# Norm stages of a graph network: one more 128x256 product behind each sum on TensorE, and a ring of sums of three pairs

## The chip, the core and the metric

The kernel runs on one core of a Trainium2 chip. The metric is the device time of one execution in microseconds (us): 6430.47 us is the median of three runs. TensorE appears as PE in the views (its weight loads as PEld), VectorE as DVE, ScalarE as ACT, GpSimd as POOL, SyncE as SP. The granted clock of TensorE is a share of full speed: 1.00 is 2.4 GHz, 0.50 is 1.2 GHz.

## The reference, cut to what matters

A layer of graph convolutions with four Runge-Kutta steps, then an attention layer. There are 50000 nodes, 25000 edges sorted by their destination, and rows of 128 or 256 numbers.

```python
def _gcn_conv(x, W, b, src, dst, dinv):
    h = x @ W
    norm = dinv[src] * dinv[dst]
    agg = jax.ops.segment_sum(h[src] * norm[:, None], dst, num_segments=x.shape[0])
    agg = agg + (dinv * dinv)[:, None] * h
    return agg + b
def f(z):
    z1 = _gcn_conv(z, Wf1, bf1, src, dst, dinv)
    z1 = _l2norm(z1)
    return _gcn_conv(z1, Wf2, bf2, src, dst, dinv) + z
k1 = f(x)
k2 = f(x + 0.5 * k1)
k3 = f(x + 0.5 * k2)
k4 = f(x + k3)
x = x + (k1 + 2.0 * k2 + 2.0 * k3 + k4) / 6.0
return _gcn_conv(x, W2, b2, src, dst, dinv)
...
x = _layernorm(x + _L0_gnn_ref(...), axis=-1)
x = _layernorm(x + _L1_gnn_ref(...), axis=-1)
```

Each `segment_sum` over 25000 edges becomes a row of small products: a 0/1 matrix that says which edges of a tile of 128 belong together (`sums_all`) times the 128 gathered rows of the tile.

## The kernel before, in words

The program is a row of stages with a barrier between them: preparation, a local pass over nodes without edges, then `first_stage`, and then by turns five norm stages (`norm_stage`, r = 0 to 4) and four mix stages (`mix_stage`, r = 0 to 3), and at the end the attention. Each norm and mix stage goes over the same 196 edge tiles, two at a time: 98 pairs. A norm stage with r = 0 to 3 has rows of 256 numbers; r = 4 (the final one) has rows of 128. In the timing, norm stage r = 0 lies at about 2088 to 2443 us, r = 1 at 2804 to 3160, r = 2 at 3521 to 3876, r = 3 at 4239 to 4682 and r = 4 at 4998 to 5290.

Work of a norm stage for pair j, tiles i = 0 and 1:

- POOL gathers the rows of both tiles from HBM into `c_rows`, a ring of four pairs (`gather_step`, L1398, two indirect DMAs); the gather of pair j waits until the sums of pair j-4 are done. Every second pair POOL also makes an inverse root (`invert`, L1735).
- SP issues the loads of `c_degs`, `c_own` and, in r = 1, 2 and 4, of one more table, in r = 3 of three more (`load_others`, L1718).
- DVE adds the last row of the sum before to the first row of the tile (`carry_step`, L1390), since a node's edges can run over a tile's border. This is the chain of the stage: the carry of tile t needs the sum of tile t-1, and the sum of tile t needs its carry.
- PE makes the sum (`add_up`): first a bias product without a wait on the carry (L1752, a single pass in the trace), then a wait for `carried`, then the 128x256 product with `sums_all` (L1754, 32-bit floats, two passes in the trace). The two accumulate in one PSUM bank. The banks are used in turn: tile 2j+i has bank (2j+i) mod 8, four pairs.
- DVE takes the pair's sums out of PSUM and adds the own rows (`add_own`, L1832) in the turn behind, clamps (L1845), and in r = 1 to 3 scales and adds an earlier table (`add_t`, L1859); ACT squares (L1773), in r = 0 also scales, and stores the pair.

DVE takes its work in the order in which it is written: carry of tile 0, `add_own` of the pair before, carry of tile 1, then the rest.

Of the kernel before, what the change touches and what calls it, by code (L numbers as in the profile page):

```python
# [13 lines left out]
D, H2 = 128, 256  # L14
# [1272 lines left out]
def coupled_stages(nc, a, S, counts, m):  # L1287
# [9 lines left out]
    with ctx:  # L1297
# [25 lines left out]
        for r in range(4):  # L1323
            norm_stage(nc, S, counts, m, r)
            if r < 3:
                mix_stage(nc, S, counts, m, r)
        mix_stage(nc, S, counts, m, 3)
        norm_stage(nc, S, counts, m, 4)


def two(tile, s, w):

    return tile[:, s, 0:2 * w].rearrange("p (i c) -> p i c", i=2)
# [18 lines left out]
def spread_turn(nc, S, m, line):  # L1352

    for k, tiles_ in enumerate((P, TE - P)):
        last = nc.tensor.transpose(m["psum"][7][0:tiles_, k * P:(k + 1) * P], line[:, k * P:k * P + tiles_],
                                   m["ident"][:])
    last.then_inc(S["degs_turned"], 1)


def spread_high(nc, act, S, m, begun):  # L1360

    act.wait_ge(S["degs_turned"], begun + 1)
    for k, tiles_ in enumerate((P, TE - P)):
        last = nc.scalar.activation(m["c_deg_hi"][0:tiles_, k, :], m["psum"][7][0:tiles_, k * P:(k + 1) * P], ACT.Copy)
    last.then_inc(S["degs_split"], 1)
# [11 lines left out]
def bias_of(m, name):  # L1377
    return m["bias_rows"][:, BIAS_AT[name][0]:BIAS_AT[name][1]]


def carry_step(nc, dve, S, m, st, before, w, i, j):


    p0, t = (0, 96)[i], 2 * j + i
    if t == 0:
        dve.sem_inc(S["carried"], 1)  # L1386
        return
    dve.wait_ge(S["summed"], st.at("summed", t))
    rows = two(m["c_rows"], j % 4, H2)[p0:p0 + 32, i, 0:w]
    nc.vector.scalar_tensor_tensor(rows, before[p0:p0 + 32, :], m["carry"][p0:p0 + 32, t:t + 1], rows, ALU.mult, ALU.add  # L1390
                                   ).then_inc(S["carried"], 1)
# [283 lines left out]
def norm_stage(nc, S, counts, m, r):  # L1675
# [4 lines left out]
    w = D if final else H2  # L1680
# [5 lines left out]
    v, psum = nc.vector, m["psum"]  # L1686
    own, rows, sums, y, rest = (m[n] for n in ("c_own", "c_rows", "sums_all", "c_y", "c_rest"))
# [4 lines left out]
    st = Steps(counts, {"carried": 2 * pairs, "summed": 2 * pairs, "u_set": pairs, "squared": 0 if final else pairs,  # L1692
                        "clamped": pairs // 2, "inverted": pairs // 2, "done": pairs,
                        "rest_set": 2 * pairs if r == 3 else 0, "x_added": pairs if final else 0,
                        "chain": 2 * pairs if final else 0, "shifted": pairs if final else 0},
               {"gathered": (32, 4, pairs), "own_in": (16, 4, pairs), "degs_in": (16, 4, pairs),
                "others_in": (16 * len(others), 4, pairs), "stored": (16, 8, pairs)})
    READY = 7

    with nc.Block() as block:  # L1700
        @block.sync
        def _(sp):
            def load(j):
                if j >= 4:
                    sp.wait_ge(S["u_set"], st.at("u_set", j - 3))
                sp.dma_start(flat(own, j % 4, w), pair_rows(source, j)).then_inc(S[st.sem("own_in", j)], 16)

            def load_degs(j):
                if j >= 4:
                    sp.wait_ge(S["summed"], st.at("summed", 2 * j - 6))  # L1710
                sp.dma_start(degs[0:3, j % 8, :].bitcast(F32), m["kap_tab"][:, j * 2 * P:(j + 1) * 2 * P]
                             ).then_inc(S[st.sem("degs_in", j)], 16)

            def load_others(j):
                if j >= 4:
                    sp.wait_ge(S["x_added" if final else "done"], st.at("x_added" if final else "done", j - 3))
                for n, table in enumerate(others):
                    sp.dma_start(flat(zs[n], j % 4, w), pair_rows(table, j)).then_inc(S[st.sem("others_in", j)], 16)  # L1718

            if r == 0:  # L1720
                spread_out(sp, S, m, m["kap_tab"], 1)
            late = 3 if final else 6
            for turn in range(pairs + late):
                if turn < pairs:
                    load_degs(turn)
                    load(turn)
                if others and 0 <= turn - late < pairs:
                    load_others(turn - late)
# [15 lines left out]
        @block.tensor  # L1744
        def _(pe):
            def add_up(j, i):
                out = psum[(2 * j + i) % 8][:, 0:w]
                if i == 0:
                    pe.wait_ge(S[st.sem("degs_in", j)], st.landed("degs_in", j))
                    if j >= 4:  # L1750
                        pe.wait_ge(S["u_set"], st.at("u_set", j - 3))
                nc.tensor.matmul(out, degs[:, j % 8, i * P:(i + 1) * P], bias_of(m, bias), start=True, stop=False)  # L1752
                pe.wait_ge(S["carried"], st.at("carried", 2 * j + i + 1))
                nc.tensor.matmul(out, sums[:, 2 * j + i, :], two(rows, j % 4, H2)[:, i, 0:w], start=False, stop=True  # L1754
                                 ).then_inc(S["summed"], 1)

            if r == 0:
                pe.wait_ge(S["kappa_set"], 3)
                spread_turn(nc, S, m, m["c_kappa"])
            for j in range(pairs):  # L1760
                add_up(j, 0)
                add_up(j, 1)

        @block.scalar
        def _(act):
# [11 lines left out]
            def scale(j):  # L1777
                act.wait_ge(S["inverted"], st.at("inverted", j // 2 + 1))
                for i in range(2):
                    part = two(y, j % 8, H2)[:, i, :]  # L1780
                    last = nc.scalar.activation(part, part, ACT.Copy, scale=inv[:, j % 8, i:i + 1])
                last.then_inc(S["done"], 1)

            def normalise(j):
                act.wait_ge(S["shifted"], st.at("shifted", j + 1))
                for i in range(2):
                    part = two(y, j % 8, D)[:, i, :]
                    last = nc.scalar.activation(part, part, ACT.Identity, bias=m["c_shift"][:, j % 2, i:i + 1],
                                                scale=inv[:, j % 8, i:i + 1])
                last.then_inc(S["done"], 1)  # L1790

            def store(j):
                act.wait_ge(S["done"], st.at("done", j + 1))
                act.dma_start(pair_rows(target, j), flat(y, j % 8, w)).then_inc(S[st.sem("stored", j)], 16)

            if r == 0:
                spread_high(nc, act, S, m, 1)
            for turn in range(pairs + READY + 1):
                if r == 0 and 0 <= turn - READY < pairs:
                    scale(turn - READY)  # L1800
                if final and 0 <= turn - READY < pairs:
                    normalise(turn - READY)
                if 0 <= turn - READY < pairs:
                    store(turn - READY)
# [6 lines left out]
        def _(dve):  # L1811
# [9 lines left out]
            def carry(j, i):  # L1821
                if i == 0:
                    dve.wait_ge(S[st.sem("gathered", j)], st.landed("gathered", j))
                carry_step(nc, dve, S, m, st, m["psum"][(2 * j + i - 1) % 8][:, 0:w], w, i, j)

            def add_own(j):
                dve.wait_ge(S["summed"], st.at("summed", 2 * j + 2))
                dve.wait_ge(S[st.sem("own_in", j)], st.landed("own_in", j))
                if j >= 8:
                    dve.wait_ge(S[st.sem("stored", j)], st.landed("stored", j - 8))  # L1830
                for i in range(2):
                    last = v.scalar_tensor_tensor(two(y, j % 8, w)[:, i, :], psum[(2 * j + i) % 8][:, 0:w],  # L1832
                                                  m["lead"][:, 2 * j + i:2 * j + i + 1], two(own, j % 4, w)[:, i, :],
                                                  ALU.mult, ALU.add)
                last.then_inc(S["u_set"], 1)
# [1056 lines left out]
```

## Time and profile before

| what | value |
|---|---|
| median of three runs | 6430.47 us (6430.21 to 6433.66) |
| the profiled execution | 6431.79 us, of which the span from the first to the last instruction is 6429.9 us |
| mean granted TensorE clock over the span | 0.809 |
| PE busy | 5150.1 us (80%) |
| DVE busy | 4720.9 us (73%) |
| POOL busy | 3923.0 us (61%) |
| ACT busy | 2819.0 us (44%) |

A busy share is a mean over stages that have different limits, so the table says where to look and not what bounds. PE's time counts a product from its start to its modelled end, in which the next one may already stream; two products that overlap count once.

### The profile page before, as it was taken

What the parts mean: (1) busy time and instruction counts of PE and PEld (TensorE: products, weight loads), DVE (VectorE), ACT (ScalarE), POOL (GpSimd) and SP (SyncE); (2) the same over time, 40 slices, a digit from 0 to 9 for tenths busy, and PEclk for the clock granted to TensorE, in tenths of its full rate; (3) what the DMA queues carried; (4) which work ended last, traced back from release to release, by engine and by line L of the source; (5) the groups of instructions that cost most, each with busy time, mean ns of one, the idle gap of its engine ahead of it and who ended that gap; (6) DMA issues with size and microseconds to landing.
All of it is one profiled execution on the core that took longest, in us unless ns stands there. A gap on an engine that the chain in (4) does not pass through costs nothing. (4 is left out here: it accounts for less than half of the span.)

```text
span 6429.9 us, 101948 instructions
## 1 busy us (share of the span) xinstructions
PE 5150.1 (80%) x25772; PEld 4128.5 (64%) x25772; DVE 4720.9 (73%) x14274; ACT 2819.0 (44%) x8831; POOL 3923.0 (61%) x3976
## 2 busy tenths in 40 slices
PE   7499999995777778987799778976679558967776
PEld 3389999994766446854487446853368447755654
DVE  8467777775665456867687776878878788888886
ACT  7167777773444553322233222322223236644442
POOL 1277777777554665557655765555556776566664
PEclk9699999997999557965599558965589559989897
DMA  0289988874554667988898888989989555534342
GB/s 2 43 218 261 262 254 258 263 234 129 158 163 156 209 216 258 323 264 287 263 324 283 285 288 280 323 294 341 341 268 282 165 163 162 160 124 122 122 124 79
DMA packets 930902, 1406.59 MB, mean 219 GB/s; under 512 B 157981, under 2 KB 453981, under 8 KB 930355
## 3 DMA queue, kind: packets, MB, share of 16 engines
q1 hardware_dynamic: 664979, 898.20, 43.7%
q0 software_dynamic: 138368, 296.57, 17.1%
q10 hardware_dynamic: 127008, 205.58, 8.7%
q8 instruction: 215, 3.52, 0.2%
q14 instruction: 332, 2.72, 0.1%
HBM read 852.92 MB, written 547.19 MB: 218 GB/s over the span
## 5 line engine op out<-in xcount | busy, mean ns | idle before, releaser
L1390 DVE SCALAR_TENSOR_TENSOR c_rows<-bank,carry,c_rows 32x256 f32<-32x256 f32 (+2 forms) x1950 | 888.6, 456 | 899.2 <-PE bank L1754 506.0
L1754 PE MATMUL bank<-c_rows,sums_all 128*128 128x256 f32 (+1 forms) x1960 | 1112.4, 671 | 532.7 <-DVE c_rows L1390 516.1
L1398 POOL DMA_INDIRECT c_rows<-y_tab,src_pair x784 | 757.0, 966 | 602.2 <-PE bank L1754 382.4
L1754 PEld LDWEIGHTS bank<-c_rows,sums_all 128*128 128x128 f32 x1960 | 489.8, 310 | 965.9 <-DVE c_rows L1390 948.3
L1398 POOL DMA_INDIRECT c_rows<-t_tab,src_pair x784 | 741.1, 945 | 519.8 <-PE bank L1982 360.6
L1773 ACT ACTIVATE c_squares<-c_y,c_root 128x256 f32<-128x256 f32 x784 | 391.7, 500 | 1022.8 <-DVE c_y L1859 779.9
L1752 PE MATMUL bank<-bias_rows,c_degs 128*128 128x256 f32 (+1 forms) x980 | 695.6, 710 | 26.7 <-DMA c_degs<-kap_tab 26.7
L2025 ACT ACTIVATE c_xt<-bank 128x512 f32<-128x512 f32 x392 | 234.1, 597 | 906.2 <-PE bank L1991 906.2
L760 PE MATMUL bank<-w_mix,lxt 128*128 128x256 f32 x2400 | 607.3, 381 | 1.9 <-ACT lxt L1029 1.9
L760 PE MATMUL bank<-w_mix,c_xt 128*128 128x256 f32 x2352 | 605.9, 380 | 0.0
L761 PE MATMUL bank<-bias_rows,two_r 128*128 128x256 f32 (+1 forms) x1400 | 595.2, 427 | 0.0
L1982 PE MATMUL bank<-c_rows,sums_all 128*128 128x256 f32 x1568 | 498.6, 400 | 106.3 <-DVEq L1386 81.8
L761 PE MATMUL bank<-bias_rows,c_degs 128*128 128x256 f32 (+1 forms) x1372 | 578.0, 423 | 0.0
L2527 POOL DMA_INDIRECT out_dram<-fl_y,node_of x396 | 394.3, 996 | 243.2 <-DVE fl_y L2845 147.2
L760 PEld LDWEIGHTS bank<-w_mix,c_xt 128*128 128x128 f32 x2352 | 424.8, 191 | 45.9
L760 PEld LDWEIGHTS bank<-w_mix,lxt 128*128 128x128 f32 x2400 | 413.0, 191 | 42.9 <-ACT lxt L1029 3.1
L1048 ACT ACTIVATE lsquares<-ly 128x256 f32<-128x256 f32 x800 | 324.4, 408 | 162.7 <-DVE ly L1219 160.6
L1752 PEld LDWEIGHTS bank<-bias_rows,c_degs 128*128 128x128 f32 x980 | 329.1, 336 | 98.4 <-DMA c_degs<-kap_tab 28.0
L1832 DVE SCALAR_TENSOR_TENSOR c_y<-bank,lead,c_own 128x256 f32<-128x256 f32 (+1 forms) x980 | 390.3, 434 | 2.2 <-PE bank L1754 2.1
L760 PE MATMUL bank<-w_first,c_z 128*128 128x256 f32 (+1 forms) x1176 | 301.4, 357 | 101.1 <-DVE c_y L1653 101.1
L1982 PEld LDWEIGHTS bank<-c_rows,sums_all 128*128 128x128 f32 x1568 | 245.5, 194 | 152.5 <-DVEq L1386 84.7
L2072 DVE SCALAR_TENSOR_TENSOR c_y<-bank,c_scale,c_rest 128x256 f32<-128x256 f32 (+1 forms) x784 | 317.4, 447 | 27.2 <-PE bank L761 15.2
(388 smaller groups left out, 13010.8 us busy)
## 6 DMA issues: line engine op xcount, KB each, us to landing
c_z<-t_tab SPq DMA_DIRECT2D x490, 256.0 KB
y_tab<-ly SPq DMA_DIRECT2D x400, 256.0 KB
t_tab<-lt SPq DMA_DIRECT2D x400, 256.0 KB
c_own<-y_tab SPq DMA_DIRECT2D x392, 256.0 KB
t_tab<-c_y ACTq DMA_DIRECT2D x392, 256.0 KB
c_own<-t_tab SPq DMA_DIRECT2D x392, 256.0 KB
c_z<-y_tab SPq DMA_DIRECT2D x294, 256.0 KB
y_tab<-c_y ACTq DMA_DIRECT2D x294, 256.0 KB
```

Of the source, the lines that this page charges most:

```text
L760: nc.tensor.matmul(out, x(k), w(k), start=(k == 0), stop=False)
L761: return nc.tensor.matmul(out, bias[0], bias[1], start=False, stop=True)
L1048: last = nc.scalar.activation(squares[:, squared[0] % 2, i, :], source(j, i), ACT.Square, scale=scale, accum_out=ss[:, turn % 4, at:at + 1])
L1390: nc.vector.scalar_tensor_tensor(rows, before[p0:p0 + 32, :], m["carry"][p0:p0 + 32, t:t + 1], rows, ALU.mult, ALU.add).then_inc(S["carrie ...
L1398: pool.indirect_dma_start(out=two(m["c_rows"], j % 4, H2)[:, i, 0:w], out_offset=None, in_=source, in_offset=bass.IndirectOffsetOnAxis(ap= ...
L1752: nc.tensor.matmul(out, degs[:, j % 8, i * P:(i + 1) * P], bias_of(m, bias), start=True, stop=False)
L1754: nc.tensor.matmul(out, sums[:, 2 * j + i, :], two(rows, j % 4, H2)[:, i, 0:w], start=False, stop=True).then_inc(S["summed"], 1)
L1773: last = nc.scalar.activation(m["c_squares"][:, i, :], two(y, j % 8, H2)[:, i, :], ACT.Square, scale=root[:, 2 * j + i:2 * j + i + 1], acc ...
L1832: last = v.scalar_tensor_tensor(two(y, j % 8, w)[:, i, :], psum[(2 * j + i) % 8][:, 0:w], m["lead"][:, 2 * j + i:2 * j + i + 1], two(own, ...
L1982: nc.tensor.matmul(psum[j % 2][:, i * H2:(i + 1) * H2], sums[:, 2 * j + i, :], two(rows, j % 4, H2)[:, i, :], start=True, stop=True).then_ ...
L2072: last = v.scalar_tensor_tensor(two(y, j % 8, w)[:, i, :], psum[4 + j % 2][:, i * H2:i * H2 + w], m["c_scale"][:, 2 * j + i:2 * j + i + 1] ...
L2527: pool.indirect_dma_start(out=m["out"], in_=y[:, j % 4, i, :], in_offset=None, out_offset=bass.IndirectOffsetOnAxis(ap=m["node_of"][:, t:t ...
```

## The change

Behind each sum in the norm stages PE gets one more product of 128x128 by 128x256 (`ident` times the first 256 columns of `w_mix`, both 32-bit floats that stand in SBUF), with no wait and no semaphore of its own. It writes PSUM bank 6, which nobody reads in these stages. To leave bank 6 (and 7) aside, the sums' ring shrinks from eight banks to six, so from four pairs to three: the bias product of pair j now waits until `add_own` of pair j-3 has read its banks, where it was pair j-4. The extra product is 256 columns wide in every norm stage, the final one too.

```diff
+    FILL = H2
...
             def add_up(j, i):
-                out = psum[(2 * j + i) % 8][:, 0:w]
+                out = psum[(2 * j + i) % 6][:, 0:w]
                 if i == 0:
                     pe.wait_ge(S[st.sem("degs_in", j)], st.landed("degs_in", j))
-                    if j >= 4:
-                        pe.wait_ge(S["u_set"], st.at("u_set", j - 3))
+                    if j >= 3:
+                        pe.wait_ge(S["u_set"], st.at("u_set", j - 2))
                 nc.tensor.matmul(out, degs[:, j % 8, i * P:(i + 1) * P], bias_of(m, bias), start=True, stop=False)
                 pe.wait_ge(S["carried"], st.at("carried", 2 * j + i + 1))
                 nc.tensor.matmul(out, sums[:, 2 * j + i, :], two(rows, j % 4, H2)[:, i, 0:w], start=False, stop=True
                                  ).then_inc(S["summed"], 1)
+                nc.tensor.matmul(psum[6][:, 0:FILL], m["ident"][:], m["w_mix"][:].rearrange("p k n -> p (k n)")[:, 0:FILL],
+                                 start=True, stop=True)
...
-                carry_step(nc, dve, S, m, st, m["psum"][(2 * j + i - 1) % 8][:, 0:w], w, i, j)
+                carry_step(nc, dve, S, m, st, m["psum"][(2 * j + i - 1) % 6][:, 0:w], w, i, j)
...
-                    last = v.scalar_tensor_tensor(two(y, j % 8, w)[:, i, :], psum[(2 * j + i) % 8][:, 0:w],
+                    last = v.scalar_tensor_tensor(two(y, j % 8, w)[:, i, :], psum[(2 * j + i) % 6][:, 0:w],
```

PE's order before, in norm stage r = 0 at pairs 3 and 4 (one row for each product; `bank<-bias_rows,c_degs` is the bias product, `bank<-c_rows,sums_all` the sum; the numbers are those of the PSUM banks, and a row names the semaphores that the instruction waits for):

```order
L1752 MATMUL bank6<-bias_rows,c_degs 128x256 [waits u_set,degs_in3]
L1754 MATMUL bank6<-c_rows,sums_all 128x256 [waits carried]
L1752 MATMUL bank7<-bias_rows,c_degs 128x256
L1754 MATMUL bank7<-c_rows,sums_all 128x256 [waits carried]
L1752 MATMUL bank0<-bias_rows,c_degs 128x256 [waits u_set,degs_in0]
L1754 MATMUL bank0<-c_rows,sums_all 128x256 [waits carried]
L1752 MATMUL bank1<-bias_rows,c_degs 128x256
L1754 MATMUL bank1<-c_rows,sums_all 128x256 [waits carried]
```

After a sum, PE makes the next bias product at once and then waits for the carry. PE's order now, at the same place (lines have moved by one to three):

```order
L1753 MATMUL bank0<-bias_rows,c_degs 128x256 [waits u_set,degs_in3]
L1755 MATMUL bank0<-c_rows,sums_all 128x256 [waits carried]
L1757 MATMUL bank6<-w_mix,ident 128x256
L1753 MATMUL bank1<-bias_rows,c_degs 128x256
L1755 MATMUL bank1<-c_rows,sums_all 128x256 [waits carried]
L1757 MATMUL bank6<-w_mix,ident 128x256
L1753 MATMUL bank2<-bias_rows,c_degs 128x256 [waits u_set,degs_in0]
L1755 MATMUL bank2<-c_rows,sums_all 128x256 [waits carried]
L1757 MATMUL bank6<-w_mix,ident 128x256
```

The extra product stands between a sum and the next bias product, so ahead of the place where PE waits for the carry; the banks of the sums start over behind bank 5, and DVE's, ACT's, POOL's and SP's orders are as they were.

## Rows read from the trace of the kernel before

**Rows 1.** The page: granted clock of TensorE in 40 equal slices, in tenths.

```profile
PEclk9699999997999557965599558965589559989897
```

**Rows 2.** Carries (L1390) of norm stages r = 0, 1, 3, 4: ns min/median/max, first and last start.

```profile
L1390 DVE SCALAR_TENSOR_TENSOR c_rows<-bank,carry,c_rows x195: 470/492/495, 2087.8 to 2442.8; 32x256 f32<-32x256 f32 x195
...
L1390 DVE SCALAR_TENSOR_TENSOR c_rows<-bank,carry,c_rows x195: 470/492/495, 2803.9 to 3159.6; 32x256 f32<-32x256 f32 x195
...
L1390 DVE SCALAR_TENSOR_TENSOR c_rows<-bank,carry,c_rows x195: 471/492/494, 4239.1 to 4682.4; 32x256 f32<-32x256 f32 x195
...
L1390 DVE SCALAR_TENSOR_TENSOR c_rows<-bank,carry,c_rows x195: 336/358/361, 4997.6 to 5290.0; 32x128 f32<-32x128 f32 x195
```

**Rows 3.** Windows: us, busy us (count) of PE, PEld, DVE, ACT, POOL; clock, DMA share, GB/s.

```profile
2100.00:2400.00 300.00, 235.03 (x493) 137.06 (x492) 150.03 (x369) 157.68 (x488) 200.12 (x205) 0.50 0.68 214
2820.00:3140.00 320.00, 249.99 (x524) 145.53 (x523) 231.45 (x565) 94.40 (x346) 224.46 (x219) 0.50 0.89 286
...
4260.00:4660.00 400.00, 248.16 (x520) 144.84 (x521) 341.77 (x735) 93.94 (x344) 214.48 (x217) 0.50 0.99 341
5010.00:5280.00 270.00, 160.40 (x534) 126.99 (x534) 229.45 (x1023) 76.36 (x175) 220.01 (x223) 0.50 0.58 174
2520.00:2750.00 230.00, 230.00 (x1269) 204.60 (x1269) 184.73 (x423) 78.71 (x141) 132.75 (x141) 1.00 0.97 323
1700.00:2000.00 300.00, 233.37 (x1474) 208.74 (x1472) 199.37 (x770) 147.53 (x556) 149.67 (x154) 1.00 0.52 163
5750.00:6150.00 400.00, 288.64 (x1491) 241.07 (x1489) 348.54 (x1495) 186.28 (x426) 269.51 (x268) 0.91 0.40 123
```

**Rows 4.** Timeline of r = 0: start us, us, engine, line, [idle before, releaser].

```profile
2250.72 0.47 DVE L1390 SCALAR_TENSOR_TENSOR c_rows<-bank,carry,c_rows 32x256 f32<-32x256 f32 x1 [1.19 <-PE bank L1754]
...
2251.24 1.22 PE L1754 MATMUL bank<-c_rows,sums_all 128*128 128x256 f32 x2 [0.42 <-DVE c_rows L1390]
...
2252.50 0.49 DVE L1390 SCALAR_TENSOR_TENSOR c_rows<-bank,carry,c_rows 32x256 f32<-32x256 f32 x1 [0.53 <-PE bank L1754]
...
2253.05 1.22 PE L1754 MATMUL bank<-c_rows,sums_all 128*128 128x256 f32 x2 [0.37 <-DVE c_rows L1390]
...
2254.38 0.47 DVE L1390 SCALAR_TENSOR_TENSOR c_rows<-bank,carry,c_rows 32x256 f32<-32x256 f32 x1 [1.38 <-PE bank L1754]
```

**Rows 5.** Waits of r = 1 (2820 to 3140 us): total us, times, longest.

```profile
DVE c_rows L1390 <- PE bank L1754: 86.6, 175, 1.4
```

**Rows 6.** Timeline of PE in mix stage r = 0, clock 1.00.

```profile
2651.18 1.03 PE L760 MATMUL bank<-w_mix,c_xt 128*128 128x256 f32 x4
2651.85 0.47 PE L761 MATMUL bank<-bias_rows,c_degs 128*128 128x256 f32 x1
2652.16 0.59 PE L1982 MATMUL bank<-c_rows,sums_all 128*128 128x256 f32 x2
2652.59 0.60 PE L1991 MATMUL bank<-ident,c_u 128*128 128x128 f32 x4
```

**Rows 7.** Timeline of PE at the start of mix stage r = 0, clock 0.50.

```profile
2474.98 1.91 PE L760 MATMUL bank<-w_mix,c_xt 128*128 128x256 f32 x4
...
2476.91 1.05 PE L1982 MATMUL bank<-c_rows,sums_all 128*128 128x256 f32 x2
```

**Rows 8.** Windows of 5 us: a rise in mix stage r = 0, a fall in the attention.

```profile
2475.00:2480.00 5.00, 5.00 (x19) 4.14 (x19) 1.48 (x4) 1.12 (x2) 1.46 (x2) 0.64 0.44 144
5800.00:5805.00 5.00, 2.79 (x16) 2.12 (x14) 4.64 (x22) 2.58 (x6) 3.00 (x3) 1.00 0.45 137
5805.00:5810.00 5.00, 4.52 (x17) 3.89 (x18) 4.38 (x19) 1.81 (x4) 3.19 (x4) 0.66 0.51 157
```

**Rows 9.** Timeline of POOL in r = 4.

```profile
5150.72 0.95 POOL L1398 DMA_INDIRECT c_rows<-g_tab,src_pair  x1 [0.30 <-issue]
```

**Rows 10.** Timeline of DVE in r = 1.

```profile
2952.53 0.47 DVE L1390 SCALAR_TENSOR_TENSOR c_rows<-bank,carry,c_rows 32x256 f32<-32x256 f32 x1 [0.40 <-PE bank L1754]
```

**Rows 11.** Timeline of DVE in r = 3.

```profile
4455.54 0.49 DVE L1390 SCALAR_TENSOR_TENSOR c_rows<-bank,carry,c_rows 32x256 f32<-32x256 f32 x1 [0.53 <-PE bank L1754]
```

## The prediction, made before the changed kernel ran

> **What bounds the kernel now.** I read the clock line of the page first: TensorE's granted clock falls to 0.5 in five stretches and stands near full speed between them [rows 1]. The windows put names to them: the norm stages run at 0.50, the mix stages between them at 1.00 [rows 3]. So the second thing to read is what a norm stage waits for, and how long a pair of tiles takes. First and last carry of a stage are 194 steps, 97 pairs, apart [rows 2]: r = 0 takes 355.0/97 = 3.66 us a pair, r = 1 takes 355.7/97 = 3.67 (r = 2 lies at the same pace), r = 3 takes 4.57, r = 4 takes 3.01.
>
> That r = 0 and r = 1 have the same pace, with DMA shares of 0.68 and 0.89 and 50% and 72% DVE busy [rows 3], says that neither DMA nor the load of DVE sets it. The timeline shows what does [rows 4]: carry at 2250.72, its sum at 2251.24 for 1.22, the next carry at 2252.50, its sum at 2253.05 for 1.22, the next carry at 2254.38. That is 3.66 us, of which the two sums are 2.44. DVE stands idle 0.53 us before the one carry and 1.38 before the other, both times until the sum is done. In r = 1 the rest of DVE's work fills the larger gap to 0.40 [rows 10], and its carries wait on PE 175 times in 320 us, 86.6 us in all [rows 5]. Norm stages 0 to 2 are thus bound by a chain in which a sum at 1.2 GHz is two thirds.
>
> In r = 3 DVE waits 0.53 us a pair for a sum [rows 11], and DMA is at 0.99 and 341 GB/s [rows 3]: two limits close to each other. In r = 4 POOL is busy 220.01 of 270 us, and has an issue gap of 0.30 us before a gather [rows 3, 9]; 223 instructions are 89 pairs (two gathers and half an inverse root each), whose 178 gaps come to 53 us. 220 + 53 is the whole window: r = 4 is bound by POOL, at 3.01 to 3.03 us a pair.
>
> **The change part by part.** *The extra product.* 196 tiles in five stages make 980 products of two passes. PE's new need for a tile is a sum, an extra product and a bias product. The mix stage shows just this load back to back: two products and a bias take 2652.16 - 2651.18 = 0.98 us at 1.00 [rows 6] and 2476.91 - 2474.98 = 1.93 us at 0.50 [rows 7]; one product alone is 2652.59 - 2652.16 = 0.43 at 1.00. The extra product needs no wait, so it starts behind the sum, while DVE makes the carry, and the next bias product stands behind it. PE's need for a pair is 1.96 us at 2.4 GHz and 3.86 us at 1.2 GHz, against 3.66 us that a pair takes now.
>
> *What that does to the clock.* At 1.2 GHz the need is above the pair's time, so PE has no gap left. A PE without a gap is what stood before the clock rose in the mix stage (5.00 of 5.00 us busy, mean clock 0.64 while it changes) [rows 8]. It fell, in the attention, behind a window in which PE was busy 2.79 of 5 us [rows 8]. Between these lie both states: first stage, busy 233.37 of 300 us, held 1.00, and r = 0, busy 235.03 of 300, held 0.50 [rows 3]; what went before decides there. After the rise a tile keeps PE busy for 0.98 us and the 0.16 that the bias product's 0.47 reaches past the next start (2651.85 + 0.47 - 2652.16) [rows 6]: 1.14 us of 1.5 to 1.6, so 3.6 of any 5 us, well above the 2.79 that stood before a fall. I take it that the clock rises within some microseconds of each norm stage's start and stays up in r = 0 to 2.
>
> *What a sum then costs.* At 1.00 the same product takes 0.59 us from start to end [rows 6], against 1.22: 0.63 less for each of two. Does the extra work hold up the next sum? Between a sum's end (2251.24 + 1.22 = 2252.46) and the start of the next (2253.05) lie 0.59 us of the carry [rows 4]. Extra product and bias (0.98 - 0.43 = 0.55) begin to stream 0.16 ahead of the sum's end (0.59 - 0.43), so they are done 0.39 behind it: hidden at 2.4 GHz, with 0.20 to spare; without that cover they would be 0.55 us a tile. DVE's own order limits the gain: before the one carry it waited only 0.53. So the chain of r = 0 drops by at most 0.53 + 0.63 to 2.50 us, that of r = 1 and r = 2 by 0.53 + 0.40 to 2.74.
>
> *What is late next.* POOL: r = 4 shows its floor at 3.01 to 3.03 us for the same two gathers and half an inverse root; a wider row doesn't lengthen POOL's instructions (200.12/205 = 0.98 us in r = 0, 220.01/223 = 0.99 in r = 4) [rows 3]. For r = 0, with DMA at 0.68, I take 3.05: 0.61 x 98 = 60 us less. r = 1 and r = 2 move the same bytes a pair as a mix stage, which takes 3.26 us (1269 passes in 230 us at 18 a pair) at a share of 0.97 and 323 GB/s, while PE is busy all the time [rows 3]. POOL gives 3.03 and this row 3.26 as ends; at 341 GB/s, as r = 3 sustains, it would be 286 x 3.67/341 = 3.08. I take 3.17: 0.49 x 98 = 48 us in each. r = 3: between 0 (DMA's share has no room) and 0.53 x 98 = 52 (nobody is seen to wait for a transfer there); PE's need is only 1.96 of more than 4 us, so the clock may come and go as in the attention, where it was 0.91 [rows 3]. I take 0.2 x 98 = 20. r = 4: POOL's floor stays, 0.
>
> *The ring of three pairs.* The bias product of pair j waits for `add_own` of pair j-3, which DVE makes in turn j-2, ahead of carries that PE needs anyway. Bounds 0 and, if it held back a bias product (0.98 - 2 x 0.43 = 0.12 at 1.00), 0.12 x 98 = 12 us a stage; I take 0. Stage ends: the last extra product is 0.85 us at most, five times: under 5 us.
>
> **The sum.** 60 + 48 + 48 + 20 = 176 us. The profiled execution took 6431.8 us, 1.3 above the median: 6431.8 - 176 = 6256, and 6255 against the median.
>
> **The rivals.** *A harder DMA limit.* r = 1 and r = 2 stop at the mix stage's 3.26, and r = 3 at its present pace: 60 + 40 + 40 = 140, so 6290. For it: shares of 0.97 and 0.99 [rows 3]. Against: no transfer is among the waits of r = 1 that I read, DVE's are on PE [rows 5].
>
> *The clock comes and goes.* With half of the time at each level, a pair takes the mean rate of 3.05 and 3.86, 3.41 in r = 0, and of 3.17 and 3.86, 3.48 in r = 1 and r = 2: 0.25 x 98 + 2 x 0.19 x 98 = 62 us less, 6369. For it: the last stages, which stand at 0.91 with PE busy 72% [rows 3]; against: before a fall their PE idles nearly half of a window of 5 us [rows 8], and here a tile's gap is 0.4 us. The Trainium skill (TensorE: Matmul & The Clock Gate, section "A second HAM failure mode: psum-queue depth-cycling") speaks against the change here: it tells of a kernel that cycles through PSUM banks, whose PE idles a little between groups of products often enough that the clock swings between its two levels. By that rule this rival would be the likeliest, at 6369; the first stage, which cycles through banks too and holds 1.00 for 300 us at 78% busy [rows 3], does not bear it out.
>
> *The clock stays at 0.50, and the extra product is a cost.* Then PE bounds r = 0 to 2 at 3.86 us a pair: 0.20 x 98 x 3 = 59 us more, 6490, slower. r = 3 (4.57) and r = 4 (half the sum, so 2 x 1.40) hide it. It decides where two products and a bias take more than 1.83 us, half a pair's time now: at 1.93 they do, at 0.98 they don't. For it: an identity as weights, nearly all zeros, may not count as work; against: the mix stage's transposes use the same identity at 1.00 [rows 6].
>
> *Nothing moves.* The sums get shorter but gathers arrive no sooner, so every stage keeps its pace: 6430. Against it stand r = 4 and the mix stage, which take 3.0 and 3.3 us a pair from the same gather ring.
>
> **Chances and range.** The forecast 0.62; the DMA limit 0.18; the swinging clock 0.08; the clock at 0.50 0.07; nothing moves 0.05. The likeliest is 6255. Its own bounds: all at POOL's floor and all of r = 3's wait gone, 62 + 2 x 63 + 52 = 240, so 6191; to the DMA limit's 6290, and with r = 0 at 3.2 (45 instead of 60) 6305. From 6200 to 6320 I leave out the last three cases, 0.20. A change of under 0.2% (13 us) can hardly be told from none here: faster 0.88, same 0.05, slower 0.07.
>
> **What would show it.** Right: PE's clock in the windows of r = 0 to 2 at 0.95 or more, sums of 0.59 us, first to last carry at 296, 307 and 307 us, POOL with gaps of 0.30 and no wait on PE in r = 0, r = 4 unchanged. Wrong: the clock at 0.50 with PE busy all the time; a mean clock near 0.75 in r = 0; or carries of r = 1 that wait for a gather to land. The mean clock over the span should go from 0.81 to above 0.9.

## The result, and the profile after

| kernel | median | runs | ratio to before, 95% interval |
|---|---|---|---|
| before | 6431.36 us | 4 | |
| changed | 6217.53 us (6208.05 to 6222.19) | 4 | 0.9665 (0.9648 to 0.9682) |

The change made the kernel 214 us faster; 6255 was forecast, and 6200 to 6320 as the range. The profiled execution took 6216.59 us, of which the span is 6214.7; the span of before was 6429.9, 215.2 more. The mean granted clock went from 0.809 to 0.937.

The page of the changed kernel, the clock in 40 slices (they are 155 us wide, 161 before):

```profile
PEclk9599999999899998999899999988799989998998
```

The five stretches at 5 [rows 1] are gone (the 5 in the second slice lies ahead of the norm stages); one of 8 8 7 is left, and it is norm stage r = 3. The windows of norm stages r = 0, 1, 3 and 4 of the changed kernel, with the columns of [rows 3]:

```profile
2100.00:2370.00 270.00, 232.20 (x910) 163.47 (x908) 165.81 (x408) 173.34 (x536) 219.54 (x225) 0.97 0.84 261
2750.00:3030.00 280.00, 223.51 (x892) 155.96 (x892) 239.14 (x577) 96.49 (x353) 230.02 (x222) 0.99 0.98 332
...
4090.00:4450.00 360.00, 248.33 (x857) 173.23 (x856) 339.16 (x728) 92.90 (x341) 231.86 (x215) 0.87 1.03 377
4800.00:5060.00 260.00, 168.94 (x861) 122.52 (x862) 224.54 (x993) 75.27 (x172) 211.32 (x217) 1.00 0.58 176
```

The clock stands at 0.97 and 0.99 where it was 0.50, and DMA moves 332 GB/s in r = 1 and 377 in r = 3, where it was 286 and 341. How it gets there, at the start of r = 0:

```profile
2086.00:2091.00 5.00, 4.01 (x11) 3.29 (x12) 1.03 (x3) 0.00 (x0) 1.59 (x3) 0.50 0.87 277
2091.00:2096.00 5.00, 4.85 (x19) 3.71 (x18) 2.96 (x7) 2.02 (x8) 3.26 (x4) 0.80 0.43 125
2096.00:2101.00 5.00, 4.71 (x21) 3.21 (x19) 3.62 (x9) 1.91 (x9) 3.49 (x5) 1.00 0.66 196
```

PE starts at 1.2 GHz, is busy 4.01 and then 4.85 of 5 us, and is at 2.4 GHz in the third window. It does not stay there without a break, as 20 us windows show:

```profile
2130.00:2150.00 20.00, 18.33 (x75) 12.81 (x74) 13.07 (x33) 13.15 (x42) 16.05 (x17) 1.00 0.87 260
...
2190.00:2210.00 20.00, 17.86 (x67) 12.86 (x68) 12.72 (x31) 13.13 (x42) 16.23 (x17) 0.91 0.83 254
```

Of the 13 such windows from 2110 to 2370 us eight read 1.00 and five 0.91: short falls that the mean of 0.97 contains. First and last carry of r = 0, 1, 2, 3 and 4, which answer to [rows 2]:

```profile
L1390 DVE SCALAR_TENSOR_TENSOR c_rows<-bank,carry,c_rows x195: 470/492/494, 2088.5 to 2378.2; 32x256 f32<-32x256 f32 x195
...
L1390 DVE SCALAR_TENSOR_TENSOR c_rows<-bank,carry,c_rows x195: 470/492/494, 2739.7 to 3043.6; 32x256 f32<-32x256 f32 x195
...
L1390 DVE SCALAR_TENSOR_TENSOR c_rows<-bank,carry,c_rows x195: 470/492/495, 3406.2 to 3707.8; 32x256 f32<-32x256 f32 x195
...
L1390 DVE SCALAR_TENSOR_TENSOR c_rows<-bank,carry,c_rows x195: 470/492/494, 4071.2 to 4473.0; 32x256 f32<-32x256 f32 x195
...
L1390 DVE SCALAR_TENSOR_TENSOR c_rows<-bank,carry,c_rows x195: 336/358/360, 4785.3 to 5075.1; 32x128 f32<-32x128 f32 x195
```

Last less first: 289.7, 303.9, 301.6, 401.8 and 289.8 us, against 355.0, 355.7, 355.4, 443.3 and 292.4 (r = 2 of before from 3521.0 to 3876.4). The differences are 65.3, 51.8, 53.8, 41.5 and 2.6: together 215.0 of the 215.2 by which the span is shorter. All of the gain lies in the norm stages.

The chain in r = 0 of the changed kernel, first DVE's timeline, then PE's, which answer to [rows 4]:

```profile
2250.53 0.49 DVE L1390 SCALAR_TENSOR_TENSOR c_rows<-bank,carry,c_rows 32x256 f32<-32x256 f32 x1
2251.88 0.47 DVE L1390 SCALAR_TENSOR_TENSOR c_rows<-bank,carry,c_rows 32x256 f32<-32x256 f32 x1 [0.86 <-PE bank L1755]
2252.28 0.85 DVE L1835 SCALAR_TENSOR_TENSOR c_y<-bank,lead,c_own 128x256 f32<-128x256 f32 x2
2253.17 0.49 DVE L1390 SCALAR_TENSOR_TENSOR c_rows<-bank,carry,c_rows 32x256 f32<-32x256 f32 x1
```

```profile
2251.08 0.70 PE L1755 MATMUL bank<-c_rows,sums_all 128*128 128x256 f32 x2
2251.61 0.59 PE L1757 MATMUL bank<-w_mix,ident 128*128 128x256 f32 x2
2251.86 0.47 PE L1753 MATMUL bank<-bias_rows,c_degs 128*128 128x256 f32 x1
2252.41 0.48 PE L1755 MATMUL bank<-c_rows,sums_all 128*128 128x256 f32 x1
```

A sum takes 0.70 us from start to end where it took 1.22 (the last row has only the first of its sum's two passes, as the view ends there). The extra product and the bias follow it, and the next sum starts at 2252.41, 0.06 behind the end of its carry (2251.88 + 0.47): the extra work doesn't hold it up. In one place DVE now passes from carry to `add_own` to carry with no wait for PE at all. The waits of r = 0 (2086 to 2382 us) say what is late instead:

```profile
DVE c_rows L1390 <- PE bank L1755: 63.0, 66, 8.5
DVE c_rows L1390 <- DMA c_rows<-y_tab,src_pair: 53.3, 38, 2.8
...
POOL c_rows L1398 <- issue: 47.3, 172, 0.3
...
POOL c_rows L1398 <- PE bank L1755: 9.4, 18, 3.1
```

Carries still wait for sums, 66 times in 195, but now 38 times for a gather too. POOL hardly waits for anybody (9.4 us for sums): its work, 219.54 of the 270 us in the window above, and its issue gaps fill nearly all of its time. So gathers come late because POOL issues them one after the other without a break.

### The profile page after: what moved, and what is told of

It reads as the page before. It is cut to its first block and busy times, and to the rows that moved or that the text cites. A ratio compares the mean times of both kernels' runs of the same rounds, so it can differ in the third digit from the quotient of the medians.

```text
span 6214.7 us, 105873 instructions
## 1 busy us (share of the span) xinstructions
PE 5075.5 (82%) x27732; PEld 4201.5 (68%) x27732; DVE 4728.6 (76%) x14274; ACT 2817.1 (45%) x8831; POOL 3943.8 (63%) x3976
## 5 line engine op out<-in xcount | busy, mean ns | idle before, releaser
L1390 DVE SCALAR_TENSOR_TENSOR c_rows<-bank,carry,c_rows 32x256 f32<-32x256 f32 (+2 forms) x1950 | 888.3, 456 | 620.7 <-PE bank L1985 263.2
L1398 POOL DMA_INDIRECT c_rows<-y_tab,src_pair x784 | 801.4, 1022 | 382.3 <-issue 183.5
L1755 PE MATMUL bank<-c_rows,sums_all 128*128 128x256 f32 (+1 forms) x1960 | 671.9, 426 | 390.1 <-DVE c_rows L1390 340.1
L1755 PEld LDWEIGHTS bank<-c_rows,sums_all 128*128 128x128 f32 x1960 | 306.1, 196 | 671.4 <-DVE c_rows L1390 649.6
L1757 PE MATMUL bank<-w_mix,ident 128*128 128x256 f32 x1960 | 618.6, 399 | 0.0
L761 PE MATMUL bank<-bias_rows,c_degs 128*128 128x256 f32 (+1 forms) x1372 | 578.6, 423 | 0.0
L1753 PE MATMUL bank<-bias_rows,c_degs 128*128 128x256 f32 (+1 forms) x980 | 469.0, 479 | 27.1 <-DMA c_degs<-kap_tab 27.1
L1757 PEld LDWEIGHTS bank<-w_mix,ident 128*128 128x128 f32 x1960 | 379.4, 202 | 49.0
L1985 PEld LDWEIGHTS bank<-c_rows,sums_all 128*128 128x128 f32 x1568 | 245.6, 194 | 151.3 <-DVEq L1386 83.1
```

What stands on the lines that cost most here:

```text
L761: return nc.tensor.matmul(out, bias[0], bias[1], start=False, stop=True)
L1398: pool.indirect_dma_start(out=two(m["c_rows"], j % 4, H2)[:, i, 0:w], out_offset=None, in_=source, in_offset=bass.IndirectOffsetOnAxis(ap= ...
L1757: nc.tensor.matmul(psum[6][:, 0:FILL], m["ident"][:], m["w_mix"][:].rearrange("p k n -> p (k n)")[:, 0:FILL], start=True, stop=True)
L1985: nc.tensor.matmul(psum[j % 2][:, i * H2:(i + 1) * H2], sums[:, 2 * j + i, :], two(rows, j % 4, H2)[:, i, :], start=True, stop=True).then_ ...
```

## The experiments

All times are medians; ratios are to runs of the kernel before on the same chip. The stage times below are last less first carry in the profiled execution, in us.

| kernel | r = 0 | r = 1 | r = 2 | r = 3 | r = 4 | median | ratio (95%) |
|---|---|---|---|---|---|---|---|
| before | 355.0 | 355.7 | 355.4 | 443.3 | 292.4 | 6431.36 | |
| changed | 289.7 | 303.9 | 301.6 | 401.8 | 289.8 | 6217.53 | 0.9665 |
| ring alone | 355.1 | 355.8 | 355.4 | 443.1 | 293.5 | 6431.09 | 1.0002 |
| 32 columns | 355.1 | 355.8 | 355.4 | 443.1 | 293.1 | 6429.62 | 0.9997 |
| 128 columns | 288.5 | 302.5 | 302.6 | 416.5 | 292.7 | 6234.01 | 0.9685 |
| 512 columns | 290.6 | 303.4 | 305.0 | 393.8 | 289.7 | 6207.77 | 0.9646 |
| r = 0 to 2 alone | 288.9 | 303.4 | 304.1 | 443.2 | 294.6 | 6266.26 | 0.9735 |
| changed, no inverse | 257.0 | 276.7 | 277.6 | 402.5 | 256.2 | 6095.72 | 0.9474 |
| before, no inverse | 355.7 | 356.4 | 356.2 | 443.3 | 275.3 | 6413.64 | 0.9966 |
| r = 3 with two tables | 289.3 | 302.6 | 304.4 | 399.5 | 289.8 | 6220.53 | 0.9669 |
| root on ScalarE, 512 | 273.6 | 281.2 | 282.2 | 394.3 | 257.9 | 6117.62 | 0.9508 |
| root on ScalarE, 256 and 512 | 258.0 | 278.3 | 279.6 | 393.2 | 256.6 | 6096.90 | 0.9474 |

### Is it the clock?

The ring of three pairs without the extra product:

```diff
-                nc.tensor.matmul(psum[6][:, 0:FILL], m["ident"][:], m["w_mix"][:].rearrange("p k n -> p (k n)")[:, 0:FILL],
-                                 start=True, stop=True)
```

> The ring of three pairs without the extra product. Clock theory (the whole gain comes from TensorE's clock, the ring costs and gives nothing): norm stages stay at a granted clock of 0.50 and 3.66 us a pair, the time is 6431 within 13 us. Rival (the shorter ring itself gives or takes something): off by more than 13 us; if each pair's bias product were held back, 12 us a stage more, up to 60.

6431.09 us, 1.0002 (0.9992 to 1.0011), every norm stage at 0.50 and within 1.2 us of before. The window of r = 0:

```profile
2100.00:2400.00 300.00, 235.00 (x493) 137.03 (x493) 149.91 (x370) 158.63 (x490) 200.39 (x206) 0.50 0.68 215
```

The ring by itself neither gives nor takes anything at 1.2 GHz. At 2.4 GHz there is no kernel with the longer ring to compare with.

The extra product with 32 columns in place of 256:

```diff
-    FILL = H2
+    FILL = 32
```

> The extra product is 32 columns wide in place of 256: an instruction pair with its weight loads, but an eighth of the streaming. Clock theory: a tile's need at 1.2 GHz is 0.85 + 0.11 + 0.24 = 1.2 us of 1.83, PE keeps its gaps, the clock stays at 0.50 in the norm stages and the time is 6431 within 13 us. Rival (any instruction in the gap does it, through keeping PE's queue or weights moving): clock up, 6215 to 6260.

6429.62 us, 0.9997 (0.9988 to 1.0007). The instructions of the change all stand there, with their weight loads, and nothing moved. Its window of r = 0:

```profile
2100.00:2370.00 270.00, 270.00 (x738) 204.31 (x739) 135.09 (x333) 142.30 (x440) 180.43 (x185) 0.50 0.68 215
```

PE is busy 270.00 of 270 us, where the expectation had gaps, and the clock is 0.50. So neither an instruction in the gap nor a PE that the profile shows as busy all the time is enough to raise the clock, and the time stays with the clock.

The extra product with 128 columns:

```diff
-    FILL = H2
+    FILL = D
```

> The extra product is 128 columns wide, half of the change's. A tile's need at 1.2 GHz is 0.85 + 0.43 + 0.24 = 1.52 us of 1.83 with gaps left; at 2.4 GHz 0.76 of 1.5. Clock theory: whatever the clock does, the time follows it stage by stage; I expect that it rises and holds in r = 0 to 2 (3.0 to 3.2 us a pair) and is up for a smaller part of r = 3 than the 0.87 of the change, 6215 to 6260. Rival (the whole gap has to be filled): clock stays at 0.50 in r = 0 to 2, 6400 or more.

6234.01 us, 0.9685 (0.9669 to 0.9702). Windows of r = 0, r = 3 and r = 4 with 128 columns:

```profile
2100.00:2370.00 270.00, 196.05 (x910) 149.12 (x909) 166.10 (x410) 173.33 (x536) 219.40 (x225) 0.97 0.85 262
4090.00:4450.00 360.00, 248.14 (x819) 187.56 (x818) 324.46 (x697) 89.56 (x328) 208.48 (x206) 0.68 1.02 363
...
4815.00:5080.00 265.00, 224.08 (x872) 198.50 (x872) 224.47 (x999) 75.50 (x172) 215.81 (x219) 0.50 0.58 173
```

Half the columns give the same clock and time in r = 0, with PE busy 73% of it. In r = 3 the clock is 0.68 and the stage 416.5 us, between 443 and 402. In r = 4 it stays at 0.50 and the stage takes 292.7 us, 2.9 more than at 1.00: that stage hardly depends on the clock.

The extra product with 512 columns:

```diff
-    FILL = H2
+    FILL = 2 * H2
```

> The extra product is 512 columns wide, twice the change's: a tile's need at 2.4 GHz is 0.43 + 0.86 + 0.12 = 1.41 us, under the 1.5 of a tile, but it ends later than the carry: 0.98 of work that begins 0.16 to 0.27 ahead of the sum's end, against 0.59 until the next sum could start, so 0.1 to 0.25 us later a tile. Cover theory: r = 0 (chain 2.50 + 0.2 to 0.5 against POOL's 3.0), r = 3 and r = 4 hide it, r = 1 and r = 2 (2.74 + 0.2 to 0.5 against 3.1) lose up to 0.1 us a pair: 6215 to 6240. Rival (the extra product is on the path): 0.43 x 196 = 84 us more in each of r = 0 to 2, 6400 or more.

6207.77 us, 0.9646 (0.963 to 0.9662). That is under the 6215 to 6240 expected: twice the extra work costs next to nothing in r = 0 and r = 1 and 3.4 us in r = 2, and r = 3, which was to stay, is 8 us shorter. The windows of r = 0 and r = 3:

```profile
2100.00:2370.00 270.00, 258.96 (x904) 158.26 (x904) 165.53 (x406) 174.58 (x540) 219.86 (x225) 1.00 0.84 262
4090.00:4450.00 360.00, 268.91 (x875) 152.70 (x874) 345.06 (x741) 95.02 (x348) 220.21 (x220) 1.00 1.04 384
```

r = 3 now holds 1.00. By columns (32, 128, 256, 512) its clock is 0.50, 0.68, 0.87 and 1.00 and its time 443, 416, 402 and 394 us. To see whether 512 beats 256 as a whole, both ran once more beside each other, five times each:

> The change itself once more, beside the next kernel on the same chip: 6217 within 8 us.

> The extra product 512 columns wide once more, in more rounds. In the first look it held the clock at 1.00 in r = 3, where 256 columns hold 0.87, and r = 3 took 394 us against 402. Clock theory: 8 to 10 us less than 256 columns, 6205 to 6211. Rival (that was chance): the intervals of the two lie over each other by more than half.

256 columns: 6214.23 us, 0.9664 (0.9651 to 0.9677). 512 columns: 6210.67 us, 0.9653 (0.964 to 0.9667). r = 3 is 400.7 and 394.1, as before, but the two intervals lie over each other by 16 of 26 or 27 ten-thousandths: by what was set down ahead, the difference in the whole time is not shown.

The extra product in r = 0 to 2 alone:

```diff
-                nc.tensor.matmul(psum[6][:, 0:FILL], m["ident"][:], m["w_mix"][:].rearrange("p k n -> p (k n)")[:, 0:FILL],
-                                 start=True, stop=True)
+                if r < 3:
+                    nc.tensor.matmul(psum[6][:, 0:FILL], m["ident"][:], m["w_mix"][:].rearrange("p k n -> p (k n)")[:, 0:FILL],
+                                     start=True, stop=True)
```

> The extra product only in r = 0, 1 and 2. Clock theory, stage by stage: r = 3 goes back from 402 to 443 us and r = 4 from 290 to 292.5, the others stay: 6217 + 41 + 3 = 6261. Rival (part of the gain of r = 3 comes from elsewhere, the shorter ring or what is left over from the stage before): r = 3 under 435 us.

6266.26 us, 0.9735 (0.9719 to 0.9752). r = 3 is back at 443.2 with the clock at 0.50, r = 4 at 294.6:

```profile
4090.00:4490.00 400.00, 248.19 (x519) 144.89 (x519) 341.66 (x734) 93.61 (x345) 215.98 (x218) 0.50 0.99 341
```

The gain is made stage by stage: r = 3 gets none of it from the norm stages ahead.

### What bounds the norm stages now?

The change without POOL's inverse root, and the kernel before without it:

```diff
-                nc.gpsimd.tensor_tensor(inv[:, s:s + 2, :], ss[:, s:s + 2, :], m["c_neg_half"][:], ALU.pow
-                                        ).then_inc(S["inverted"], 1)
+                pool.sem_inc(S["inverted"], 1)
```

> The change, and POOL leaves the inverse root out in the five norm stages (it only raises the semaphore; rows are scaled with old values, so this part of the computation is not done). POOL theory (after the change r = 0, 1, 2 and 4 stand at POOL's floor of two gathers and half an inverse root, 3.0 us a pair): the floor falls to 2 x (0.95 + 0.30) = 2.50; r = 0 goes from 290 to about 252 us (its chain then 2.6), r = 1 and r = 2 from 303 to about 275 (DVE's order 2.8), r = 4 from 290 to 251 to 270; r = 3 stays. Some 6080 to 6130. Rival (DMA is the floor of r = 1 and r = 2, share 0.98): these two stay at 300 to 304 us, 6140 to 6170. Rival (the chain is still the floor): nothing moves, 6217.

> The kernel before, and POOL leaves the inverse root out in the five norm stages (this part of the computation is not done). Chain theory (before the change r = 0 to 2 were bound by carry and sum at 1.2 GHz, r = 4 by POOL): r = 0, 1, 2 stay at 355 us, r = 3 at 443, r = 4 goes from 292 to 251 to 285: 6390 to 6425. Rival (POOL had a part in the pace of r = 0 to 2 before): each of them shorter by more than 5 us.

6095.72 us, 0.9474 (0.9458 to 0.9489), and 6413.64 us, 0.9966 (0.9954 to 0.9979). After the change, taking half an inverse root a pair from POOL shortens r = 0 by 33 us, r = 1 by 27, r = 2 by 24 and r = 4 by 34. Before the change the same edit leaves r = 0 to 2 where they were, 0.7 to 0.8 us longer, and shortens only r = 4, by 17. So POOL was not the bound of r = 0 to 2 before and is after; the bound has moved from the chain to POOL. The window of r = 1 without the inverse, after the change:

```profile
2715.00:2980.00 265.00, 232.19 (x932) 161.52 (x932) 246.19 (x598) 100.75 (x369) 175.42 (x186) 1.00 1.01 361
```

r = 1 moves its bytes in 276.7 us in place of 303.9, at 361 GB/s and a share of 1.01. The share of 0.98 in the changed kernel was not a limit.

r = 3 with two tables in place of three, in the changed kernel:

```diff
-    before = [[], [0], [1], [0, 1, 2], []][r]
+    before = [[], [0], [1], [0, 1], []][r]
...
-                v.scalar_tensor_tensor(rest[:, j % 2, :], zs[2][:, j % 4, :], 0.75, rest[:, j % 2, :], ALU.mult, ALU.add)
+                v.scalar_tensor_tensor(rest[:, j % 2, :], zs[1][:, j % 4, :], 0.75, rest[:, j % 2, :], ALU.mult, ALU.add)
```

> The change, and norm stage r = 3 loads two tables in place of three (the third is replaced by the second in the arithmetic, so this part of the computation is not the reference's): five transfers of 256 KB a pair in place of six, DVE's work the same. DVE theory (r = 3 is bound by DVE's order, busy 94%): its first to last carry stays at 402 us within 6. Rival (DMA, at 377 GB/s and a share of 1.03): it falls by 10 us or more, to as little as 385.

6220.53 us, 0.9669 (0.9653 to 0.9685); r = 3 takes 399.5 us, 2.3 less. Its window:

```profile
4090.00:4450.00 360.00, 249.40 (x855) 174.10 (x855) 338.71 (x728) 93.12 (x341) 232.67 (x216) 0.86 0.95 313
```

A sixth of the bytes is gone (313 GB/s against 377) and the pace is nearly the same, so it isn't DMA; without the inverse root r = 3 takes 402.5 us, so it isn't POOL. DVE is busy 338.71 of 360 us in the one and 339.16 in the other, and its carries have all but stopped waiting for sums. The waits of r = 3 before (4270 to 4660 us) and in the changed kernel (4090 to 4450 us):

```profile
DVE c_rows L1390 <- PE bank L1754: 45.2, 85, 0.5
...
DVE c_rows L1390 <- PE bank L1755: 6.2, 13, 0.5
```

What is left as the bound of r = 3 is DVE's own list of work.

### A version that beats both

If POOL is the bound, the inverse root should leave it without being dropped. ScalarE takes the root, VectorE the reciprocal, POOL's `invert` goes, and the extra product is 512 columns wide:

```diff
+            def take_root(g):
+                act.wait_ge(S["clamped"], st.at("clamped", g + 1))
+                s = 2 * g % 8
+                nc.scalar.activation(inv[:, s:s + 2, :], ss[:, s:s + 2, :], ACT.Sqrt).then_inc(S["norm_root"], 1)
...
+            def invert(g):
+                dve.wait_ge(S["norm_root"], st.at("norm_root", g + 1))
+                s = 2 * g % 8
+                v.reciprocal(inv[:, s:s + 2, :], inv[:, s:s + 2, :]).then_inc(S["inverted"], 1)
```

> 512 columns, and the inverse root leaves POOL: ScalarE takes the root of the sums of squares, VectorE the reciprocal, every second pair. POOL theory: stage times as without the inverse (257, 277, 277 and 256 us in r = 0, 1, 2, 4), plus up to 0.16 us of DVE every second pair (8 us a stage), r = 3 at 394 to 402: 6090 to 6125. Rival (the new hand-over from DVE to ACT and back is on the path): r = 0 and r = 1 over 285 us, 6150 or more.

6117.62 us, 0.9508 (0.9495 to 0.9521): within what the POOL theory gave, but r = 0 is 273.6 us where 257 to 265 were due. The window and PE's timeline of r = 0 show why:

```profile
2100.00:2320.00 220.00, 220.00 (x783) 137.08 (x783) 150.22 (x393) 153.77 (x504) 147.91 (x157) 1.00 0.88 279
```

```profile
2200.25 0.59 PE L1746 MATMUL bank<-c_rows,sums_all 128*128 128x256 f32 x2
2200.68 1.02 PE L1748 MATMUL bank<-w_mix,ident 128*128 128x512 f32 x2
2201.14 0.68 PE L1744 MATMUL bank<-bias_rows,c_degs 128*128 128x256 f32 x1
2201.66 0.59 PE L1746 MATMUL bank<-c_rows,sums_all 128*128 128x256 f32 x2
```

Sum to sum is 2201.66 - 2200.25 = 1.41 us, with PE busy all the time: 2.82 a pair, and 273.6/97 = 2.82 is what r = 0 takes. With POOL out of the way the 512 columns themselves are the bound. So the next kernel has them in r = 3 alone:

```diff
-    FILL = 2 * H2
+    FILL = 2 * H2 if r == 3 else H2
```

> The inverse root on ScalarE and VectorE as before, and the extra product 512 columns wide in r = 3 alone, 256 in the other norm stages. With 512 columns r = 0 took 273.7 us, 2.82 a pair, with PE busy all the time: sum, product and bias are 1.41 us a tile, 2.82 a pair. Theory (in r = 0 the extra product itself had become the bound): r = 0 goes to 255 to 265 us, r = 1 and r = 2 stay within 5 us of 281, r = 3 stays at 394 and r = 4 at 258: 6095 to 6110. Rival (the hand-over between DVE and ACT is what r = 0 waits for): r = 0 stays at 270 us or more, 6115 to 6122.

6096.90 us, 0.9474 (0.9461 to 0.9487), r = 0 at 258.0. That is 121 us under the change. Its POOL timeline in r = 0 shows what bounds there now:

```profile
2200.95 0.95 POOL L1398 DMA_INDIRECT c_rows<-y_tab,src_pair  x1 [0.44 <-PE bank L1746]
2202.21 0.95 POOL L1398 DMA_INDIRECT c_rows<-y_tab,src_pair  x1 [0.30 <-issue]
```

POOL waits 0.44 us for a sum ahead of each pair, where in the changed kernel it had only its issue gap of 0.30. The waits of r = 0 (2100 to 2330 us) agree:

```profile
DVE c_rows L1390 <- PE bank L1746: 56.3, 85, 0.9
...
POOL c_rows L1398 <- PE bank L1746: 39.0, 86, 0.9
...
DVE c_rows L1390 <- DMA c_rows<-y_tab,src_pair: 1.6, 2, 0.8
```

Carries wait for sums and hardly for gathers: the chain of carry and sum is ahead of POOL again, at 258.0/97 = 2.66 us a pair. The inverse root is made in this kernel, and r = 0 takes nearly what it took without the root (257.0): it was the root's time on POOL that counted.

## Why the prediction was right, and where it was off

**The clock** was forecast to rise within some microseconds and to hold in r = 0 to 2. It did: 0.80 on average in the second 5 us window of r = 0, then 0.97 and 0.99 with short falls. That the time hangs on it is shown from both sides: 32 columns leave the clock and the time as they were, 128 columns raise the clock and shorten the time. The argument for it was weaker than it looked: "a PE without a gap is what stood before the clock rose" holds in the mix stage [rows 8] and fails with 32 columns, where PE shows no gap at 0.50. A busy row of the trace includes the modelled ends of products. The width of the extra product told more: with 32, 128, 256 and 512 columns r = 0 ran at 0.50, 0.97, 0.97 and 1.00. With 128 columns, which by the working ahead of that run leave PE a gap at 1.2 GHz (1.52 us of 1.83), the clock rose too, so that PE has no gap left was not the reason. Nor does any run show that "what went before decides there": with 32 and with 128 columns r = 0 follows the same first stage.

**The swinging clock** came true in one stage. r = 0 to 2 cycle through six PSUM banks, with gaps, and fall only for short moments (0.97 to 0.99, not the half of the time that the rival took): the Trainium skill's section "A second HAM failure mode: psum-queue depth-cycling" (TensorE: Matmul & The Clock Gate) is not borne out for them. r = 3 has the same six banks and swings (0.87). There PE waits longer for DVE (4090 to 4450 us; in r = 0, from 2086 to 2382, it was 30.1 us, 37 times):

```profile
PE bank L1755 <- DVE c_rows L1390: 107.2, 85, 1.9
```

With 512 columns the banks are the same and r = 3 holds 1.00, so it is not the banks that make it swing. What the runs bear out is the Trainium skill's section "What's actually happening" (the same page), that half speed is the resting state and activity lifts it: more columns in r = 3, more of the time at 2.4 GHz.

**The sum** was taken at 0.59 us, from products in the middle of a stream; behind a wait it takes 0.70. That cost nothing in r = 0 to 2, since POOL was the floor.

**r = 0, r = 1 and r = 2** were forecast at 60, 48 and 48 us less and gave 65.3, 51.8 and 53.8, at 2.99, 3.13 and 3.11 us a pair against 3.05 and 3.17. The floor was named right: POOL, as shown by the kernels without the inverse root. The value for r = 1 and r = 2 had been moved up from POOL's 3.03 towards a DMA limit that isn't there: without the inverse they go to 2.85. That 3.17 came near is luck. What makes r = 1 slower than r = 0 is POOL itself, whose instructions take 230.02/222 = 1.04 us there against 219.54/225 = 0.98: 0.06 x 2.5 = 0.15 us a pair, which is the distance from 2.99 to 3.13. "A wider row doesn't lengthen POOL's instructions" was read from r = 0 and r = 4; r = 1 stood at 224.46/219 = 1.02 already before [rows 3]. What r = 1 has and r = 0 has not is DVE's scaling (L1862). In r = 1 (POOL's and DVE's timelines) a gather that starts beside it takes 1.23 us, the next one 0.95:

```profile
2901.74 1.23 POOL L1398 DMA_INDIRECT c_rows<-y_tab,src_pair  x1 [0.19 <-issue]
2903.27 0.95 POOL L1398 DMA_INDIRECT c_rows<-y_tab,src_pair  x1 [0.31 <-issue]
...
2901.58 0.88 DVE L1862 SCALAR_TENSOR_TENSOR c_y<-c_y,c_inv,c_z 128x256 f32<-128x256 f32 x2 [0.33 <-POOL c_inv L1736]
```

Whether DVE's instruction is the cause no run shows; in r = 3 of the kernel before (4260 to 4660 us), the 86 gathers that start beside the same scaling take 1.01 us on the mean, the other 87 take 0.95. One sign that was named for wrong did appear, carries of r = 1 that wait for a gather (2735 to 3047 us):

```profile
DVE c_rows L1390 <- DMA c_rows<-y_tab,src_pair: 11.8, 20, 1.6
```

It does not tell a DMA limit from a late POOL, since a gather that is issued late lands late as well; the kernel without the inverse root does.

**r = 3** is the term that was mis-sized: 20 us forecast, 41.5 measured, of a bound of 52. The step that failed is "0 (DMA's share has no room)". Four fifths of the wait that DVE had for a sum could be won because DMA's share of 0.99 at 341 GB/s was no ceiling; it went to 1.03 at 377, and to 1.04 at 384 with 512 columns. The other reason given, a clock that comes and goes, was right and small: at 1.00 the stage gains 49.5, at 0.87 41.5. The row that nobody waited for a transfer there should have had more weight than the share.

**r = 4** was forecast unchanged, since POOL bounds it: 2.6 us less, and at 0.50 (128 columns) 292.7 us against 289.8 at 1.00. Removing half an inverse root a pair there gives 34 us after the change and 17 before: at 1.2 GHz something stood closer behind POOL, at 275.3/97 = 2.84 us a pair, which the prediction had not seen. There POOL waits for sums, so it is likely the chain; no run of its own shows it.

**The ring** was taken at 0, and is 0 at 1.2 GHz, where it could be compared.

**The sum of the terms** was 176 and the measured 215; r = 3 makes 21.5 of the 39 that lack, r = 0 to 2 together 15, r = 4 the other 2.6. The rivals "the clock stays at 0.50", "nothing moves" and "a harder DMA limit" are excluded by the stage times above.

## What to carry to other kernels

Where a chain of short products with gaps runs at half clock between stages at full clock, compare what a product takes in the two: the difference, times the products on the chain, is the most that the clock costs, and work that nobody reads can buy it back if it fits into the gap at full clock. Its width has to be tried: here 32 columns did nothing, and 128 did in r = 0 what 256 did and in r = 3 only a part of it. Bound the gain by the next engine's own pace (here POOL's two gathers and half an inverse root), read from a stage that is already bound by it; the gain of the next step lies there. A high DMA share need not be a limit: here r = 3 stood at 0.99 while its carries waited for sums, and went on to 1.04.

## What the runs showed of the hardware that was not expected

The share and rate of DMA in r = 3 rose from 0.99 and 341 GB/s to 1.04 and 384 when the sums got shorter. The Trainium skill (DMA: Bandwidth & Descriptors, section "Where 436 GB/s comes from") names about 358 GB/s, half of what it gives for the memory that two cores share, as the side that binds between HBM and SBUF; by that r = 3, at six transfers of 256 KB a pair, could not go under 6 x 262144/358 ns = 4.39 us a pair, an estimate from the page. It went to 393.8/97 = 4.06, with one core at work. The measurement decides: for a core alone the half is no bound.

PE was busy 270.00 of 270 us at a granted clock of 0.50 with 32 columns, and 196.05 of 270 at 0.97 with 128 (both in r = 0). The busy share of the profile says little about which of the two levels a stage gets.

A two-pass product of 256 columns takes 0.70 us from start to end behind a wait at full clock, and 0.59 in a stream.
